# A recommendation tower on one Trainium2 core: another start-up order, the first chunk's layer-0 blocks copied from SBUF, a ring of three in the tail

## The reference, cut to what matters

```python
e = stack([tbl_f[ids[:, f]] for f in range(39)], axis=1)      # (512, 39, 16)
def _cin_layer(X0, Xi, W, b):                                 # three of them, H = 128
    Wr = W.reshape(H, F0_, Fi)
    return einsum('hjk,bjd,bkd->bhd', Wr, X0, Xi) + b[None, :, None]
X0 = Xi = e
for W, b in Ws:
    Xi = _cin_layer(X0, Xi, W, b)
    res.append(Xi.sum(axis=2))
h = concat([concat(res, 1), dense_ctx], 1)                    # (512, 3*128 + 16)
h = maximum(h @ W_top1 + b_top1, 0); h = maximum(h @ W_top2 + b_top2, 0)
y = h @ W_top3
```

## Time and profile before

| | us |
|---|---|
| median of 3 runs | 657.85 (655.26 to 657.89) |
| the profiled execution | 650.86 |
| its span, first to last instruction | 649.1 |
| PE busy in the span | 616.1 (95%) |
| DVE busy in the span | 579.1 (89%) |

### The profile page before, as it was taken

How to read it: one execution, slowest core, us unless ns; L and a number is a source line. 1 busy time by engine, 2 the same in 40 slices (tenths; PEclk the granted TensorE clock), 3 DMA queues, 4 the chain that set the end, 5 groups by cost and what they waited for, 6 DMA issues and landing times.

```text
span 649.1 us, 14322 instructions
## 1 busy us (share of the span) xinstructions
PE 616.1 (95%) x2591; PEld 477.4 (74%) x2591; DVE 579.1 (89%) x1230; ACT 557.4 (86%) x1763; POOL 467.5 (72%) x437
## 2 busy tenths in 40 slices
PE   0399999999999999999999999999999999999998
PEld 0167787878878787878787887878787878776573
DVE  0578999999999999999999999999999999999780
ACT  2177999999999999999999999999999999998572
POOL 6779988889797979898798979797987666220000
DMA  8543405050413223140405041322314050000100
GB/s 223 145 108 72 124 9 144 11 139 20 115 45 93 66 66 94 31 129 7 137 18 141 18 121 38 94 65 65 95 36 122 6 149 2 12 2 17 66 1 0
DMA packets 44274, 46.16 MB, mean 71 GB/s; under 512 B 20896, under 2 KB 27264, under 8 KB 44233
## 3 DMA queue, kind: packets, MB, share of 16 engines
q1 hardware_dynamic: 38626, 43.59, 23.7%
q0 software_dynamic: 5120, 1.32, 2.3%
q10 hardware_dynamic: 487, 0.74, 0.4%
HBM read 44.30 MB, written 1.31 MB: 70 GB/s over the span
## 4 chain that ended last, share of the span: by engine, by line
PE 86%; DVE 5%; DMA 3%; issue 3%; SPq 1%; DVEq 1%; ACT 1%; ACTq 0%
PE ya L513 12%; PE ya L514 12%; PE ya L515 12%; PE yd L513 9%; PE yd L515 8%; PE yd L514 8%; PE misc L496 5%; PE acc L485 4%; PE acc L484 4%; PE acc L486 3%; DVE chain L636 2%; DMA w<-in_w 2%; PE acc L489 1%; DMA tiles<-x_rows 1%; PE yd L587 1%
## 5 line engine op out<-in xcount | busy, mean ns | idle before, releaser
L764 ACT ACTIVATE prods<-ya,x0t 128x128 f32<-128x128 f32 x1472 | 453.3, 511 | 37.2 <-PE ya L515 36.5
L636 DVE SCALAR_TENSOR_TENSOR chain<-yd,x0t,chain 128x128 f32<-128x128 f32 x768 | 218.4, 343 | 1.8 <-PE yd L515 1.6
L391 POOL DMA_INDIRECT emb<-in_tables,rows x160 | 157.4, 984 | 35.6 <-issue 24.9
L513 PE MATMUL ya<-w1h,x1h 128*128 128x512 f32 (+1 forms) x384 | 166.5, 434 | 1.1 <-DVE x1l L704 1.1
L426 POOL TENSOR_TENSOR prod0l<-prod,prod0h 120x512 fp32r<-120x512 f32 x98 | 127.7, 1303 | 48.5 <-ACT prod0h L773 47.6
L514 PE MATMUL ya<-w1l,x1h 128*128 128x512 f32 (+1 forms) x384 | 147.6, 384 | 0.0
L515 PE MATMUL ya<-w1h,x1l 128*128 128x512 f32 (+1 forms) x384 | 147.4, 384 | 0.0
L305 POOL TENSOR_TENSOR prod<-tiles,x0a 120x512 f32<-120x512 f32 x105 | 137.1, 1306 | 8.6 <-DMA tiles<-x_rows 3.3
L651 DVE TENSOR_REDUCE x2t<-prods 128x128 f32<-128x1792 f32 x64 | 129.2, 2019 | 2.4 <-DVE chain L636 0.3
L651 DVE TENSOR_REDUCE prods<-prods 128x128 f32<-128x1536 f32 x64 | 111.8, 1746 | 0.0
L513 PE MATMUL yd<-w1h,x1h 128*128 128x512 f32 x256 | 102.4, 400 | 2.6 <-DVE prods L636 2.2
(11 more groups left out here) (99 smaller groups left out, 610.0 us busy)
## 6 DMA issues: line engine op xcount, KB each, us to landing
tiles<-x_rows SPq DMA_DIRECT2D x236, 78.0 KB
x0a<-x_rows SPq DMA_DIRECT2D x45, 80.0 KB
emb<-in_tables,rows POOLq DMA_INDIRECT x160
w<-in_w SPq DMA_DIRECT2D x3, 832.0 KB, 11.0
w<-in_w SPq DMA_DIRECT2D x13, 192.0 KB, 2.4
tiles<-x_rows SPq DMA_DIRECT2D x32, 42.0 KB
x<-x_rows SPq DMA_DIRECT2D x16, 78.0 KB
x<-x_rows SPq DMA_DIRECT2D x16, 77.8 KB
```

The costliest lines, as they stand in the source:

```text
L391: pool.indirect_dma_start(emb[:, c % 2, fo * D:(fo + 1) * D], None, a["tables"], bass.IndirectOffsetOnAxis(ap=rows[:, c, fo:fo + 1].bitcas ...
L513: pe.matmul(out, x1h[:, c % 2, xs], w1h[:, cols], start=True, stop=False)
L636: dve.scalar_tensor_tensor(out, product, x, run if step else b1[:, :], ALU.mult, ALU.add).then_inc(yd_used, 1)
L764: mm = act.activation(prods[:, :, slot_of(q) + i], ya[(NA * g + k) % YA][:, i * H:(i + 1) * H], ACT.Copy, scale=turned(c)[:, g * F1 + j:g ...
```

## The change

Start-up: W1 is issued right behind the ids, ahead of `const`, W0 and the biases; `first_row` goes to ACT's queue. POOL adds the table starts for chunk 0 alone before the first gather and for the other chunks behind chunk 0's ten gathers. DVE clears `x0a`, waits for the layout, then adds W0's halves. ACT scales `bias` later. Layer 0 of chunk 0: SP loads the first of the three copies of X0, waits until it has landed, and only then issues the other two; `x0a` and all seven tiles of chunk 0 are copied from that landed copy (partitions 0 to 38 of `x0`) rather than from the scratch tensor; `x0a`'s three parts are 39 rows each. PE runs three extra float32 matmuls (`WARM`) into an unused `ya` tile as soon as X0 has been stored. Last chunk: the sum over dimensions goes from DVE to POOL, as four adds that halve the terms in place. Tail: the ring has three buffers, so `whole` is 4 and `split` 35.

```diff
+WARM = 3
-RING = 4
+RING = 3
@@
+        def x0_rows(x, row, count):
+            return (x0 if x == 0 else chunk_rows(x))[row:row + count, :]
         def load_x0a(engine, x):
+            count = F if x == 0 else R0
             for u in range(3):
-                engine.dma_start(x0a[u * R0:(u + 1) * R0, :], chunk_rows(x)[0:R0, :]).then_inc(x0a_in, 16)
+                engine.dma_start(x0a[u * R0:u * R0 + count, :], x0_rows(x, 0, count)).then_inc(x0a_in, 16)
@@ load_tile
-                engine.dma_start(tiles[a:b, i % L0_TILES, :],
-                                 chunk_rows(x)[row:row + b - a, :]).then_inc(tile_in[i % L0_TILES], 16)
+                engine.dma_start(tiles[a:b, i % L0_TILES, :], x0_rows(x, row, b - a)).then_inc(tile_in[i % L0_TILES], 16)
@@ load_x0
                 for g in range(XB):
+                    if x == 0 and g == 0:
+                        sp.dma_start(x0[0:F, :], chunk_rows(0)[0:F, :]).then_inc(x0_first, 16)
+                        sp.wait_ge(x0_first, 16)
+                        continue
@@ SP
             sp.dma_start(rows[:, :, :], a["ids"]).then_inc(ids_in, 16)
-            sp.dma_start(first_row[:, :], a["first_row"]).then_inc(ids_in, 16)
+            (W1 in three parts, then const, w0ab, b1, b0, b2)
             store_x0(0)
-            sp.wait_ge(scratch_in, 2 * 16)
+            load_x0(0)
             load_tile(sp, 0, 0)
             load_tile(sp, 0, 2)
-            load_x0(0)
@@ POOL
+            def sum_dims_last():
+                pool.wait_ge(x1h_ready, CHUNKS)
+                terms, count = x1[:, :].rearrange("p (g d b) -> p g d b", g=GROUPS, d=D), D
+                while count > 2:
+                    count //= 2
+                    pool.tensor_tensor(terms[:, :, 0:count, :], terms[:, :, 0:count, :], terms[:, :, count:2 * count, :],
+                                       ALU.add).then_inc(z_adds, 1)
+                    pool.wait_ge(z_adds, {8: 1, 4: 2, 2: 3}[count])
+                out = z[:, (CHUNKS - 1) * CB:].rearrange("p (g b) -> p g b", g=GROUPS)
+                pool.tensor_tensor(out, terms[:, :, 0, :], terms[:, :, 1, :], ALU.add).then_inc(z_sums, 1)
-            pool.tensor_tensor(rows[:, :, :], rows[:, :, :], base, ALU.add).then_inc(rows_ready, 1)
+            pool.tensor_tensor(rows[:, 0:1, :], rows[:, 0:1, :], base, ALU.add).then_inc(rows_ready, 1)
             gather(0, range(FO))
+            pool.tensor_tensor(rows[:, 1:, :], rows[:, 1:, :], base.to_broadcast([P, CHUNKS - 1, FO]), ALU.add).then_inc(rows_ready, 1)
@@ PE
+            pe.wait_ge(w1_in[0], 16)
+            pe.wait_ge(scratch_in, 2 * 16)
+            for _ in range(WARM):
+                pe.matmul(ya[YA - 1][:, :], const[:, C_ID:C_ID + P], w1_raw[:, 0:COLS], start=True, stop=True)
@@ DVE
-                                if (g, half) == SUM_DIMS:
+                                if nxt and (g, half) == SUM_DIMS:
                                     sum_dims(c)
+            dve.memset(x0a[:, :], 0.0).then_inc(x0a_clear, 1)
+            dve.wait_ge(lay_done, 1)
             dve.wait_ge(w0_in, 16)
             dve.tensor_tensor(w0[:, :, :].rearrange("p s h -> p (s h)"), w0ab[:, 0], w0ab[:, 1],
@@ ACT
+            act.dma_start(first_row[:, :], a["first_row"]).then_inc(ids_in, 16)
-            act.wait_ge(scratch_in, 2 * 16)
+            act.wait_ge(x0a_clear, 1)
+            act.wait_ge(x0_first, 16)
             load_x0a(act, 0)
```

More of the change, by code:

```diff
@@ L255, in build @@
         ones_ready = sem("ones_ready")
-        x0_in = sem("x0_in")
+        x0_in, x0_first, x0a_clear = sem("x0_in"), sem("x0_first"), sem("x0a_clear")
         lay_done, x0_ready = sem("lay_done"), sem("x0_ready")
@@ L264, in build @@
         x1h_ready, x1_first, x1_split = sem("x1h_ready"), sem("x1_first"), sem("x1_split")
-        z_sums = sem("z_sums")
+        z_sums, z_adds = sem("z_sums"), sem("z_adds")
         ya_ready, yd_ready = sem("ya_ready"), sem("yd_ready")
@@ L351, in _ @@
                              ).then_inc(w1_in[i], 16)
+            sp.dma_start(const[:, :], a["const"]).then_inc(const_in, 16)
+            sp.dma_start(w0ab, a["w0ab"]).then_inc(w0_in, 16)
+            sp.dma_start(b1[:, :], a["b1"].rearrange("(o h) -> o h", o=1).to_broadcast([P, H])
+                         ).then_inc(bias_in, 16)
+            for i, name in enumerate(("b0", "b2")):
+                sp.dma_start(bias[:, i:i + 1], a[name].rearrange("(p o) -> p o", o=1)).then_inc(bias_in, 16)
             store_x0(0)
-            sp.wait_ge(scratch_in, 2 * 16)
+            load_x0(0)
             load_tile(sp, 0, 0)
             load_tile(sp, 0, 2)
-            load_x0(0)
             for i in range(L0_TILES, T0):
@@ L429, in _ @@
             pool.wait_ge(ids_in, 2 * 16)
-            base = first_row[:, :].rearrange("p (o f) -> p o f", o=1).to_broadcast([P, CHUNKS, FO])
-            pool.tensor_tensor(rows[:, :, :], rows[:, :, :], base, ALU.add).then_inc(rows_ready, 1)
+            base = first_row[:, :].rearrange("p (o f) -> p o f", o=1)
+            pool.tensor_tensor(rows[:, 0:1, :], rows[:, 0:1, :], base, ALU.add).then_inc(rows_ready, 1)
             pool.wait_ge(rows_ready, 1)
             gather(0, range(FO))
+            pool.tensor_tensor(rows[:, 1:, :], rows[:, 1:, :], base.to_broadcast([P, CHUNKS - 1, FO]), ALU.add).then_inc(rows_ready, 1)
+            pool.wait_ge(rows_ready, 2)
             gather(1, range(1))
@@ L449, in _ @@
                         block_diagonal(c, DIAG_AFTER[i])
+                    if c == CHUNKS - 1 and i == 2:
+                        sum_dims_last()
                     if c == CHUNKS - 1 and i == 3:
@@ L468, in turn_x0 @@
             def turn_x0(c):
-                pe.wait_ge(x0_in, 16 * XB * (c + 1))
+                pe.wait_ge(x0_in, 16 * (XB * (c + 1) - 1))
                 by_group = x0[:, :].rearrange("p (n g) -> p g n", g=GROUPS)
@@ L691, in _ @@
                               ALU.add).then_inc(w0_ready, 1)
-            dve.wait_ge(lay_done, 1)
             for i in range(W1_PARTS):
@@ L797, in chunk @@
                             evacuate_x1(c + 1)
-            act.wait_ge(bias_in, 3 * 16)
-            act.mul(bias2d[:, :], bias[:, 1:2], float(D)).then_inc(bias2d_ready, 1)
+            act.dma_start(first_row[:, :], a["first_row"]).then_inc(ids_in, 16)
             for i in range(W1_PARTS):
@@ L809, in _ @@
             evacuate_x0t(0)
+            act.wait_ge(bias_in, 3 * 16)
+            act.mul(bias2d[:, :], bias[:, 1:2], float(D)).then_inc(bias2d_ready, 1)
             act.wait_ge(w0_ready, 1)
```

## The result

The changed kernel takes 662.83 us (median, 662.37 to 663.01) against 657.87 (median of the kernel before, from 655.26; one of its six executions took 3334.81, without it the median is 657.85): ratio 1.0084, 95% interval 1.0062 to 1.0105. The changed kernel is slower by a small amount that is clear of the noise, and outside the range of 654.2 to 661.8. Its profiled execution took 662.85 with a span of 661.1, 12.0 above the 649.1 of the profile before. The medians lie only 5.0 apart, because that profile lay 7.0 under its own median. So the 12.0 say where time went against the one execution that was profiled; what the other executions of the kernel before did in their 7.0 has no trace.

The account below looks back on a forecast made before the run. It took PE, busy 95% of the span, as the bound, with layer 0 of chunk 0 bound by transfers and the last chunk by DVE. Terms +1.2 − 1.1 − 0.65 = −0.55 from 657.85 gave 657.3 us, range 654.2 to 661.8.

Parts of the forecast that it names:

- First gather: Start-up, chunk 0's gather: earlier ids and a smaller add save 0.7 us, X0's store issued at 18.7.
- X0's own load: Start-up: the 78 KB load issued at 20.8 lands at 22.7; x0a issued at 22.75, 1.25 us later than before.
- The copies: Layer 0 of chunk 0: 1.92 MB copied at 172 GB/s, 11.1 us of data, layer 0 done at 37.4.
- rival 1: Layer 0 of chunk 0: copies no slower than loads from memory, SP's issuing the limit; 655.5 us, chance 0.25.
- The start-up's term: Start-up to the end of layer 0: done at 37.4 instead of 36.18, net +1.2 us, gather's 0.7 included.
- rival 2: Layer 0 of chunk 0: X0's few partitions throttle copies to 130 GB/s, +4.8 us; 660.9 us, chance 0.33.
- Run-up: PE before layer 0: three extra matmuls gain nothing, as DVE's products wait for tiles; 0.3 us at most if overrunning.
- The clock: PE in start-up and last chunk: granted clock read as 1.00; no term for a change of it.
- Last chunk: Last chunk: DVE, the bound, loses its 1.16 us reduction and PE can follow; −1.1 us, half at worst.
- Ring of three: Tail: four fields move from plain to halves, −0.8, against DVE's later start; −0.65 us taken, ring holds by 0.2.
- rival 3: Tail: the ring of three buffers starves PE, 32 fields lose about 1 us; 658.3 us, chance 0.07.
- The frame: Whole kernel: middle chunks keep their length; the change acts only on start-up, last chunk and tail.

Follow-up runs that it names:

- e1: The changed kernel with x0a and chunk 0's seven tiles loaded from memory again, chip A: 649.15 us against 652.36 for the kernel before, ratio 0.9949.
- e15: The changed kernel with chunk 0's blocks and tiles from memory, run-up kept, chip C: 649.13 us against 652.59 for the kernel before, ratio 0.9952.
- e4: The changed kernel with chunk 0's copies moving columns 0 to 255 of 512 only, same number of DMAs, chip A: 658.52 us (one execution).
- e9: The changed kernel with each chunk 0 copy split in two by columns, same bytes, chip B: 677.68 us against 656.16 for the kernel before, ratio 1.0323.
- e16: The changed kernel with chunk 0's loads from memory and without the three extra matmuls, chip C: 650.04 us, ratio 0.9962 to the kernel before.
- e3: The changed kernel without the three extra matmuls (WARM = 0), copies kept, chip A: 659.83 us, ratio 1.0106 to the kernel before.
- e6: The kernel before itself, without any edit, profiled on chip B: 655.83 us, ratio 0.999.
- e14: The changed kernel without the three extra matmuls (WARM = 0), copies kept, chip C: 659.01 us, ratio 1.0101 to the kernel before.
- e12: The changed kernel, copies kept, with eleven more extra matmuls in PE's gaps up to layer 1, chip B: 669.58 us, ratio 1.0196 to the kernel before.
- e7: The changed kernel with chunk 0's loads from memory and without the three extra matmuls, chip B: 654.92 us, ratio 0.9973 to the kernel before.
- e8: The changed kernel with chunk 0's loads from memory and a ring of four buffers, chip B: 656.44 us, ratio 1.0 to the kernel before.
- e10: The changed kernel with chunk 0's loads from memory, run-up kept, chip B: 656.67 us, ratio 0.9997 to the kernel before.
- e11: The changed kernel with chunk 0's loads from memory and three more extra matmuls around layer 0, chip B: 656.67 us, ratio 0.9996 to the kernel before.

## Why the prediction was wrong

*First gather: right.* The store was to be issued at 18.7 and was at 18.51. Little of it arrives: with loads from memory (e1, e15) DVE still waits mostly for its transfers, and layer 0 is taken 0.1 to 0.4 sooner than before.

*X0's own load: right.* `x0a` was forecast for 22.75 and issued at 22.59.

*The copies: the step that failed.* I bounded them by their data (229 or 130 GB/s, 172 taken) and took the duration of an issue, 0.37, from loads from memory, even in rival 1, which made issuing the limit. The trace had no row of a copy's issue, and I gave that unknown no bound. It is 0.75 at the median: twenty on SP alone take 17.5 to 18.9 us with the few slow ones among them, past the forecast's whole data phase of 11.1. The start-up's term was +1.2 and came out at +10.2, of which 8.3 are up to the last product. The rate seen, 116 GB/s, lies near rival 2's 130, and whoever read only that would have called rival 2 right. But the DMA engines were busy 0.49 of the time, half the bytes left the median issue as long and took only 2 to 3 us off the queue (e4), and twice the copies for the same bytes cost 15.5 us more (e9). So the rate was in the main the result of the issue, not the limit. The point from which rival 2 was to decide comes out at 165 GB/s by its own terms, not 158; nothing rests on it. The interval from `x0a` to ACT's start, 14.7 before, 14.6 forecast and 18 by rival 2, was 23.8.

The Trainium skill ("DMA: Bandwidth & Descriptors", section "Issuing engines are not separate DMA queues") calls the time in which an engine initiates a DMA usually small against the DMA itself; for these 78 KB copies it is not: 0.75 of queue each, 0.38 if two queues shared them evenly, against an estimated 78 KB / 229 GB/s = 0.35 of data at the rate of the earlier trace rows. The port rule quoted in the prediction was not what decided; whether it slows a copy at all, no run here isolates.

*Run-up: right in size, not in reason.* Forecast nothing: measured 0.4 slower with copies and 0.9 faster from memory, with intervals that overlap; the trace shows the second (layer 0 taken at 35.74, in e16 at 37.54). With copies it ends at 26.08, 3.4 before the first product. The reason given, that DVE's products wait for tiles and not for PE, already fails in the trace before, in a row between those of the earlier trace rows (first line). In e16, from memory without the run-up, four of the seven products wait for PE, 4.0 us in all (second line, the first of them); in e15 none does.

```profile
31.02 0.69 DVE L305 TENSOR_TENSOR prod<-tiles,x0a 120x512 f32<-120x512 f32 x1 [1.35 <-PE acc L489]
```

```profile
31.18 0.69 DVE L310 TENSOR_TENSOR prod<-tiles,x0a 120x512 f32<-120x512 f32 x1 [1.63 <-PE acc L509]
```

*The clock: missing.* I read a granted clock of 1.00 before and held it constant, though I had noted that two records of layer 0 take 2.04 us where the tail's take 0.89: a recorded 1.00 there does not mean full speed. The changed kernel loses 3.1 at the start of layer 1, and ACT's take of layer 0 comes 3.1 after PE's last matmul (43.32 to 46.41) where e3 has 1.2 (43.59 to 44.75). The kernel before shows such a fall on chip B too (e6), so it is not all the change's doing.

*Last chunk: right.* Forecast −1.1, measured −1.14 (e1, first matmul of layer 1 to the last sum: 558.65, before 559.79), with PE's wait nearer 1 than 2.

*Ring of three: mis-sized, −0.65 forecast and −0.2 measured.* PE takes 3.67 for the plain matmuls instead of 7.11, which saves 3.4, but the fields in halves take 3.3 more and not 4 x 0.68 = 2.7. They now pass at DVE's pace: its low halves are 692 ns each with 0.1 us idle ahead of them in all, where before DVE waited 3.3 for a buffer. I had given DVE 0.62 a field against PE's 0.68; it keeps 24.0 / 35 = 0.69. No gap at every third field: rival 3 did not occur.

*The frame: right.* Middle chunks kept their length. Summed with the measured sizes, the steps give +12.0 in the profile and, on chip C, 10.3 for the copies less 3.5 for the rest. Of that 3.5, the spans of the two profiles (649.1 and 647.2) show 1.9; the other 1.6 are in executions of the kernel before on chip C which were not profiled.

## What to carry to other kernels

Before a load is replaced by a copy within the chip, price the issue as well as the bytes: many small DMAs on one queue are a chain of issues, and where the trace has no issue of that kind it is an unknown with two ends like any other. Here a low rate with the DMA engines half idle pointed to the queue, and a run with twice the DMAs for the same bytes showed it. TensorE's clock where its full load begins is a term of its own: from the first matmul of layer 1 to the first `x2t` it is 9.9 us in the profiles that show no fall (before, e1, e14, e15, e16) and 11.4 to 17.4 in those with a fall there.

## What the runs showed of the hardware that was not expected

- A DMA from SBUF to SBUF held SP's queue for 0.75 us (median) at 512 and at 256 columns alike, 0.68 with 3 rows, one from memory 0.33; ACT's eight took 0.98 while both queues were copying. A store from SBUF to memory took 0.38 (128 partitions) or 0.51 (32).
- TensorE can stop delivering for 6 us (e6) to 9 us (e12) while its records run on for a part of it. The half clock is recorded from the end of the stop (e6) or from 3 us before it (e12), for 3 to 10 us. It is seen in consumers that wait "issue" or "remote" for tiles that the record has as done. Of the profiles with loads from memory it came in all of chip B (e6, e7, e8, e10, e11; e6 is the kernel before) and in none of chips A and C (e1, e15, e16). Of those with copies only e14 (chip C) shows none. What triggers it stays open: filling the gaps made it come earlier (e12), leaving the run-up out did not remove it in e3 and e7.
- Why the issue of a copy within SBUF takes twice as long stays open. The number of rows is not the cause (0.68 with 3, 0.74 and more with 39), nor is the source alone (the stores' 0.38 and 0.51); a copy from many partitions to many was not tried.
